# Attention and feed-forward block: q's low part on VectorE, and q's stack loaded ahead of the shift rows

## The reference

```
q = rope(layernorm(x) @ Wq.T + bq);  k = rope(ctx @ Wk.T + bk);  v = ctx @ Wv.T + bv
scores = q k^T / 4, where |i - j| <= 50, else -1e9;  p = softmax(scores)
x = x + tanh(g_xattn) * (p v @ Wo.T + bo)
x = x + tanh(g_ffn)   * ffn(layernorm(x))
```

## Time and profile before

| | |
|---|---|
| three runs, median (lowest to highest) | 1411.48 us (1404.42 to 1416.85) |
| the profiled execution's own time | 1405.53 us |
| its span, first to last instruction | 1403.8 us |
| mean granted clock of TensorE, share of full speed | 0.941 |
| busy over the span: PE, DVE, ACT, POOL | 85%, 86%, 60%, 42% |
| busy in 340 to 560 us: PE, DVE, ACT, POOL | 194.6, 201.1, 140.7, 175.0 of 220 us |
| own time less span | 1.7 us |

### The profile page before, as it was taken

One profiled execution on the slowest core, in us unless ns is written; L12 is line 12 of the kernel. 1 busy time (PEld: TensorE's weight loads), 2 busy tenths in 40 slices (PEclk: granted clock), 3 DMA queues, 4 the chain that ended last, 5 costly groups with the idle time before them and its releaser, 6 DMA issues. The chain is left out here.

```text
span 1403.8 us, 27833 instructions
## 1 busy us (share of the span) xinstructions
PE 1195.9 (85%) x8960; PEld 807.6 (58%) x8992; DVE 1202.3 (86%) x3570; ACT 837.5 (60%) x1336; POOL 587.1 (42%) x1392
## 2 busy tenths in 40 slices
PE   3367898988888888888888767999899979977998
PEld 2245676776766766666676543444333334436887
DVE  5678998999999899899989736998899989997886
ACT  2225665656666565657565545664676779993332
POOL 1127787778778787778777640000000000000000
PEclk7679999999999999999999988999999999998999
DMA  3174856566666667575757311222455455556774
GB/s 113 34 161 108 180 137 159 137 159 148 149 157 149 153 144 158 138 158 139 169 127 170 85 38 45 112 91 111 151 188 187 170 179 193 188 179 203 234 237 164
DMA packets 132369, 207.27 MB, mean 148 GB/s; under 512 B 11159, under 2 KB 97050, under 8 KB 126106
## 3 DMA queue, kind: packets, MB, share of 16 engines
q1 hardware_dynamic: 132250, 205.86, 53.6%
HBM read 125.60 MB, written 79.69 MB: 146 GB/s over the span
## 5 line engine op out<-in xcount | busy, mean ns | idle before, releaser
L596 ACT ACTIVATE probs<-psum 128x356 f32<-128x356 f32 x512 | 210.2, 464 | 246.4 <-PE psum L852 246.4
L707 DVE CUSTOM_DVE_ANT_0 psum<-psum,band 128x178 f32<-128x178 f32 x1024 | 317.2, 372 | 40.1 <-PE psum L835 38.5
L1014 PE MATMUL psum<-xnT,w_upT 128*128 (+1 forms) x1152 | 260.8, 384 | 19.1 <-DVE maxima L1238 8.8
L527 POOL TENSOR_SCALAR_AFFINE_SELECT probs<-probs 128x154 f32<-128x154 f32 (+1 forms) x512 | 214.3, 426 | 146.9 <-ACT probs L596 141.0
L835 PE MATMUL psum<-k_stack,q_stack 96*128 96x178 bf16 x1024 | 143.2, 251 | 88.0 <-issue 57.2
L1014 PEld LDWEIGHTS psum<-xnT,w_upT 128*128 128x128 f16 x1152 | 109.7, 99 | 170.0 <-issue 32.2
L536 POOL TENSOR_SCALAR_AFFINE_SELECT probs<-probs 128x254 f32<-128x254 f32 (+1 forms) x512 | 189.1, 393 | 0.0
L835 PEld LDWEIGHTS psum<-k_stack,q_stack 96*128 96x128 bf16 x1024 | 76.5, 100 | 145.4 <-issue 86.6
L707 DVE DVE_READ_ACCUMULATOR2_ANT smax<- 128x1 f32 x1024 | 142.7, 139 | 0.0
L1614 PE MATMUL psum<-w_downT,xnT 128*128 128x256 f16 x1152 | 128.1, 275 | 16.0 <-DVE xnT L1564 16.0
L1014 PE MATMUL psum<-xnT,w_gateT 128*128 (+1 forms) x576 | 125.9, 382 | 8.7 <-DVE xnT L1087 8.7
(11 more groups left out here) (189 smaller groups left out, 2283.7 us busy)
## 6 DMA issues: line engine op xcount, KB each, us to landing
k_parts_scratch<-k_parts SPq DMA_DIRECT2D x32, 384.0 KB, 2.6
q_parts_scratch<-q_parts SPq DMA_DIRECT2D x32, 384.0 KB, 2.6
k_stack<-k_parts_scratch SPq DMA_DIRECT2D x32, 384.0 KB, 5.1
q_stack<-q_parts_scratch SPq DMA_DIRECT2D x32, 384.0 KB, 6.0
gate_scratch<-g_stage SPq DMA_DIRECT2D x16, 768.0 KB, 3.3
g_in<-gate_scratch SPq DMA_DIRECT2D x16, 768.0 KB, 4.6
sig_scratch<-w_gateT SPq DMA_DIRECT2D x32, 384.0 KB, 2.3
sig_again<-sig_scratch SPq DMA_DIRECT2D x32, 384.0 KB, 3.4
```

The lines of the kernel that those rows point to most:

```text
L527: nc.gpsimd.affine_select(out=t[:, :, 0:n], in_=t[:, :, 0:n], pattern=[[0, 2], [1, n]], compare_op=ALU.is_ge, fill=0.0, base=WINDOW - off, ...
L596: nc.scalar.activation(ring_tile(probs, b, pair, c)[:].rearrange("p e j -> p (e j)"), scoreT_bank[c][:, 0:2 * SPAN], ACT.Exp, scale=DK ** ...
L707: ins = nc.vector.tensor_tensor_reduce(out=mine, in0=mine, in1=keep["band"][:, t, :], scale=1.0, scalar=-3e38, op0=ALU.add, op1=ALU.max, a ...
L1014: last = nc.tensor.matmul(bank[:], weights[wp][:, c * I + f * P:c * I + (f + 1) * P], x_parts[:, c, bass.ds(j * (2 * TILE) + xp * TILE, TI ...
```

## The change

q's low part moves from POOL's slot 5 to DVE's slot 6, ahead of that slot's maxima. In SP's stream q's stack is loaded in the iteration that stored it, right behind k's stack, and the first half of the shift rows follows it, at the end of the iteration (b1 there is what b2 is at the start of the next).

```diff
-        def low(eng, by, b, n):
-            if not b.real:
-                return
-            reached(eng, mid_ready[n], b, 1, 1)
-            by.tensor_tensor(parts[n][:, 2, :], rest[n][:], parts[n][:, 1, :], ALU.subtract)\
-                .then_inc(low_ready[n], 1)
...
             def steps(rnd, unit):            # SP
-                load_shift(Batch(rnd, unit, 2), 0)
-                load_stacks(Batch(rnd, unit, 1), "q")
                 load_x(Batch(rnd, unit, -1))
...
                 store_parts(Batch(rnd, unit, 0), "q")
                 load_stacks(Batch(rnd, unit, 0), "k")
+                load_stacks(Batch(rnd, unit, 0), "q")
+                load_shift(Batch(rnd, unit, 1), 0)
...
                     cut(Batch(rnd, unit, late), pair)        # POOL
-                    if slot == 5:
-                        low(pool, nc.gpsimd, Batch(rnd, unit, 0), "q")
...
+            def low(b, n):                   # DVE
+                if not b.real:
+                    return
+                reached(dve, mid_ready[n], b, 1, 1)
+                nc.vector.tensor_tensor(parts[n][:, 2, :], rest[n][:], parts[n][:, 1, :], ALU.subtract)\
+                    .then_inc(low_ready[n], 1)
...
                     if slot == 5:
-                        low(dve, nc.vector, b0, "k")
+                        low(b0, "k")
                         remainder(b0, "q")
+                    if slot == 6:
+                        low(b0, "q")
```

## The result

The changed kernel takes 1403.1 us (median of 19 runs, 1398.0 to 1409.9) against 1410.8 (19 runs of before, 1404.4 to 1418.2): a ratio of 0.9949, 95% interval 0.9933 to 0.9965. It is 0.5% faster; 14 us were forecast, about 7.5 came. So the two traces differ by 2.4 us only, and they serve to tell mechanisms, not the size of the gain.

The account below looks back on a forecast made before the run. DVE, busy 201 of 220 us, was taken as the bound. 22.19 + 0.36 = 22.55 against 22.97 us an iteration gave 13 us over 31 iterations, perhaps 1 more: 1411.5 - 14 = 1397 us, 8-in-10 range 1380 to 1415.

Parts of the forecast that it names:

- The wait ahead of pair 0 goes: PE's wait for q's stack ahead of pair 0's scores disappears, as q's stack DMAs go out 3.1 us earlier.
- 2.1 us to spare: Margin between q's last stack DMA landing and PE wanting it for pair 0's scores in the next iteration.
- The place of the low part costs 0.36 us: Ahead of slot 6's maxima, q's low part delays PE's chain from slot 7 to slot 1: 0.36 us an iteration.
- DVE's short wait for the output projection: Sign of a right forecast: DVE's L749 waits briefly for PE's output projection (L810).
- k_cos's longer wait: Sign of a right forecast: k_cos, first step of k's rope, waits 1.2 us or more for PE's k projection.
- DVE's account: Rival, chance 0.18: only DVE's own work counts, low part costs -0.14 us, gain 29 us, 1383 us.
- I take it as gone in all: Step crediting the whole pair 0 wait and what follows, 0.78 us an iteration, giving a 22.19 us pace.
- The port: Rival, chance 0.10: q's low part or `shift_parts` waits behind POOL cuts, up to 0.35 to 0.5 us; 1410 us.
- The shift rows: Rival, chance 0.13: shift rows queued behind q's stack land too late for pair 0's `scoresT`; 1432 us at 9.3 us landing.

Follow-up runs that it names:

- e1: Full change with SP's old order put back, so only q's low part moves to DVE's slot 6; 1402.3 us, 0.9944 of the kernel before.
- e9: e1 with q's low part behind slot 6's maxima instead of ahead of them; 1388.0 us, 0.9868 of the kernel before.
- e6: e1 plus unneeded PE work, att transposed twice in slot 7 ahead of scores of pair 4; 1389.4 us, 0.9862 of the kernel before.
- e4: Full change with k's remainder moved behind slot 4's maxima; 1393.6 us, 0.9887 of the kernel before.
- e14: Full change plus unneeded PE work, att transposed twice in slot 7; 1399.6 us, 0.9921 of the kernel before.
- e2: Kernel before with SP's new order alone, q's low part still on POOL in slot 5; 1444.8 us, 1.0243 of the kernel before.
- e3: Full change with q's low part behind slot 6's maxima instead of ahead of them; 1413.3 us, 1.0020 of the kernel before.
- e15: e12 with SP's new order on top, q's stack ahead of the shift rows; 1399.0 us, 0.9926 of the kernel before.
- e12: Kernel before with q's low part still on POOL but ahead of slot 5's cut, SP's order old; 1373.4 us, 0.9714 of the kernel before.
- e10: Kernel before with k's stack loaded ahead of q's store in SP's order, low part still on POOL; 1417.6 us, 1.0053 of the kernel before.

## Why the prediction was right, and where it was too high

The direction and the range were right, and the path in the main. The size was nearly twice what came, and the 0.5% falls among the differences under 1% that the prediction took as no change, with a chance of 0.44.

*The wait ahead of pair 0 goes:* right, but in part by luck. SP issued q's store at 13.53 us after k_cos and q's stack at 16.37, as against 13.6 and 16.2. The landing was mis-sized: 6.9 us were counted and 8.4 came, since in the new order q's stack follows closer behind k's. The 2.1 us to spare just covered it. And the credit went to the wrong half. e1 shows that SP's new order adds nothing to it; the earlier store does it, with q's stack landing in 5.9 us.

*The place of the low part costs 0.36 us:* right as a mechanism and a size (0.34 by e9 against e1). The undisturbed iteration is 22.44, where 22.55 was forecast. Of the marks named, DVE's short wait for the output projection came. k_cos's longer wait did not: its median fell from 0.98 to 0.78 us. The prediction had named a wait of 1.0 us or less as the mark of DVE's account, and this mark misled, for the 0.34 us are there.

*"I take it as gone in all":* this is the step that failed. 0.78 us an iteration was the distance from the mean to a quiet iteration of before. As the pace without the wait 22.19 was well read: in the trace of before the five iterations of 22.14 to 22.16 us have no wait of DVE for pair 0. But I took the changed kernel to run at its quietest pace throughout, and it runs at 22.93 on average and 22.44 undisturbed. Two things make up the difference. The low part ahead of the maxima opens a new idle time on PE, after which the clock falls in some iterations: about 8 of 13 us in the trace, and shown to be a cause by e6 on the old order. And DVE, freed ahead of pair 0, meets POOL's rotation (1.04 us instead of 0.75). e4, which moves k's remainder, gains 9.5 us on the full change; e14, which fills PE's idle time, gains 3, and that isn't clear of noise. I had asked what DVE would wait for next, not what the new idle time does to the clock, nor which POOL instruction now runs beside DVE's.

*DVE's account* does not decide. e9 and e1 put the same 0.68 us on DVE, and their undisturbed iterations differ by 0.34. Off PE's chain it comes near: it gives 22.19 - 0.14 = 22.05, and e9 has 22.09. *The port* was right in kind and wrong in place: q's low part never waited, k's remainder did. This agrees with the rule of the Trainium skill ("SBUF — State Buffer", "Who interferes with whom") cited in the prediction, by which the DVE instruction with two SBUF inputs that starts second waits to the end: L685 starts 0.32 us after L507 and ends 0.56 us after it, where it takes 0.69 us when nothing holds it.

*The shift rows* were the right danger. The prediction took 6.9 us for their landing, from a row of q's stack, and where PE waited for them it was 7.0 to 7.3 (e2, e3, e15), under the 8.2 from which DVE would have felt it. The full change escapes narrowly, with 8 waits of 5.8 us in all; e2, e3 and e15 don't, and all three have the new order, with q's store 1.5 to 3.9 us later.

Two things stay open: why the clock falls behind that idle time in some iterations and not in others (in e1 PE idles 0.57 us there in every iteration and the projection is slow in 6), and how much of e4's gain is k's remainder and how much the clock.

## What to carry to other kernels

When a wait is bought off, price the kernel at its average pace and not at its best, and look for the idle time and the neighbours that the new timing makes. Where loads turn round through HBM in one queue, keep the small load that a chain waits for ahead of the large ones: the other order cost 34 us in e2 and 26 in e15 against e12. And ask who can do the last step before the store sooner, on the same engine, before moving it to the one that bounds. And test the halves of a change apart: here one half gave everything and the other was a loss of 2.4% by itself.

## What was not expected of the hardware

Work without use made a kernel faster: 0.66 us of repeated transposes in each iteration took 13 us off 1402 (e6), with no output projection left at a granted clock of 0.50. On the full change the same filling gave 3 us, which isn't clear of noise (e14). And a store of 384 KB that lands in 2.6 us in the kernel before took 5.5 us when 768 KB of loads had been issued just ahead of it (e10), while 4 KB of shift rows behind q's stack held PE up by 58.7 us in 25 iterations (e2).
